# A hand-woven schedule for a two-layer graph network: seeds, round matrices, switch, clearing and loads get places in the tables

## What is computed

```python
# layer 0
mask = adj > 0
h  = relu((x @ W1a)[:, :, None, :] + (x[:, :, None, :] - x[:, None, :, :]) @ W1b + b1)
hm = einsum('bjkh,bjk->bjh', h, mask)
x  = layernorm(x + hm @ W2 + deg[..., None] * b2)
# layer 1
m   = relu(relu(x @ W1g + b1g) @ W2g + b2g)
msg = relu(adj @ m)
gi, gh = msg @ W_ih.T + b_ih, x @ W_hh.T + b_hh
r, z = sigmoid(i_r + h_r), sigmoid(i_z + h_z)
n = tanh(i_n + r * h_n)
x = layernorm(x + (1 - z) * n + z * x)
```

## Time and profile before

| | |
|---|---|
| median of three runs | 1038.85 us |
| the profiled execution's own time | 1039.86 us |
| its span, first to last instruction | 1038.2 us |
| mean granted TensorE clock | 0.95 |
| TensorE / VectorE / ScalarE / GpSimd busy | 86% / 83% / 54% / 30% |

### The profile page before, as it was taken

One profiled execution on the slowest core, in us unless ns is written; L12 is line 12 of the kernel. 1 busy time (PEld: TensorE's weight loads), 2 busy tenths in 40 slices (PEclk: granted clock), 3 DMA queues, 4 the chain that ended last, 5 costly groups with the idle time before them and its releaser, 6 DMA issues.

```text
span 1038.2 us, 25022 instructions
## 1 busy us (share of the span) xinstructions
PE 894.2 (86%) x10099; PEld 611.8 (59%) x10132; DVE 864.7 (83%) x1055; ACT 563.9 (54%) x1627; POOL 312.8 (30%) x300
## 2 busy tenths in 40 slices
PE   2778888989898998989899898989989898999874
PEld 1446666556666665666666566666666566666542
DVE  5489999898889888898988889888888988888643
ACT  3434355674656557555556656555665646555342
POOL 2101021331415142241525233142523314142341
PEclk9779999999999999999999999999999999999986
DMA  3131221222121211212121121212112221111000
GB/s 125 26 98 42 62 52 28 62 52 73 42 67 43 63 37 51 73 42 70 40 82 41 28 72 42 82 27 83 42 37 63 52 72 42 38 42 27 1 11 22
DMA packets 31426, 53.28 MB, mean 51 GB/s; under 512 B 8137, under 2 KB 16972, under 8 KB 31308
## 3 DMA queue, kind: packets, MB, share of 16 engines
q1 hardware_dynamic: 31308, 51.65, 19.3%
...
## 4 chain that ended last, share of the span: by engine, by line
PE 54%; ACT 17%; DVE 11%; issue 8%; POOL 5%; SPq 2%; another core or an unknown queue 1%; DMA 0%; POOLq 0%; DVEq 0%
PE PS L768 12%; PE PS L777 8%; DVE AC L1079 4%; DVE AC L1090 3%; PE PS L851 3%; ACT AM L1363 3%; PE PS L834 3%; PE PS L621 3%; ACT YO L1324 2%; POOL st L1469 2%; PE PS L754 2%; ACT AC L1410 2%; PE PS L642 2%; ACT AM L1364 2%; PE PS L608 2%
## 5 line engine op out<-in xcount | busy, mean ns | idle before, releaser
L1090 DVE SCALAR_TENSOR_TENSOR AC<-PS,AC 128x1152 f32<-128x1152 f32 (+1 forms) x288 | 351.4, 1220 | 73.8 <-PE PS L768 69.5
L1079 DVE SCALAR_TENSOR_TENSOR AC<-PS,AC 128x1152 f32<-128x1152 f32 (+1 forms) x288 | 350.9, 1218 | 55.1 <-PE PS L777 37.6
L768 PE MATMUL PS<-DM,VA 128*128 128x192 fp8e5 (+1 forms) x1152 | 137.6, 244 | 19.3 <-DVE AC L1079 8.2
L768 PE MATMUL PS<-DM,VB 128*128 128x192 fp8e5 (+1 forms) x1152 | 139.0, 245 | 0.0
L777 PE MATMUL PS<-DM,VB 128*64 128x192 fp8e5 (+1 forms) x1152 | 98.2, 252 | 41.1 <-DVE AC L1090 40.9
L768 PEld LDWEIGHTS PS<-DM,VA 128*128 128x128 f16 x1152 | 91.7, 101 | 40.8 <-DVE AC L1079 17.8
L1526 POOL MEMSET AC<- 128x768 f32 x32 | 23.7, 740 | 283.4 <-DVE DM L1060 268.7
L777 PEld LDWEIGHTS PS<-DM,VB 128*64 128x64 f16 x1152 | 43.5, 110 | 108.3 <-issue 50.5
L777 PE MATMUL PS<-DM,VA 128*64 128x192 fp8e5 (+1 forms) x1152 | 100.1, 255 | 0.0
L768 PEld LDWEIGHTS PS<-DM,VB 128*128 128x128 f16 x1152 | 77.5, 100 | 38.2 <-issue 3.2
L1533 POOL TENSOR_TENSOR AC<-AC,NNB 128x512 f32<-128x512 f32 x64 | 68.9, 1097 | 64.0 <-ACT AC L1410 64.0
...
## 6 DMA issues: line engine op xcount, KB each, us to landing
CW<-WM SPq DMA_DIRECT2D x128, 160.0 KB, 2.8
...
VA<-VN SPq DMA_DIRECT2D x64, 96.0 KB, 2.2
VB<-VN SPq DMA_DIRECT2D x64, 96.0 KB, 2.2
...
```

The source lines that it names most:

```text
L768: last = e.matmul(PS[:, b + i % 2, 256 * (i // 2) + cols.start:256 * (i // 2) + cols.stop], lhs[:, GRAPH[i], 0:128], d[:, i, :], start=Fal ...
L1079: e.scalar_tensor_tensor(dst, tiles(PS[:, b:b + 3, :])[:, :, cols], 0.0, dst, ALU.max, ALU.add).then_inc(s["sx"], 1)
L1090: e.scalar_tensor_tensor(dst, tiles(PS[:, b:b + 3, :])[:, :, cols], 0.0, dst, ALU.max, ALU.add).then_inc(s["sy"], 1)
```

## The change

Every piece of fixed work gets a letter or digit of its own, and the tables get a string more, for the gap ahead of B1: `0` and `1` are dgen 0 and 1 of the next quad, `2`, `3` and `4` those of this stage's, `s` seeds, `w` switch, `c` clear, `l` load. All four tables are new. Only the order of instructions in each engine's queue changes, and with it which of the two spare banks a piece gets.

```diff
--- before.py
+++ after.py
@@ -55,14 +55,15 @@
 ORDER = (
-    ("pe", "pte", "p", "te", "prt", "t", "pr", "re", "pe", "er", "pd", "pd", "pe", "pd", "pe", "d", "e", "r"),
...
+    ("ps2p3", "pe", "t", "t", "", "dtr", "e", "pdrpe", "", "ert", "pee", "ep", "4d", "p", "pre", "", "cwpd", "r", "e01"),
+    ("sp2d3", "pp", "", "t", "d", "tpp", "", "4tept", "n", "dp", "d", "p", "dc", "nld", "d0wpd", "", "epd", "p", "d1r"),
 )
...
@@ -482,8 +483,6 @@
             do("dgen", 0, 1)
             do("clear", 0)
             for t in range(NQ + 1):
-                if t < NQ:
-                    do("seeds", t)
                 link["t"] = tail(t - 2) if t > 1 else iter(())
                 if t % 2 == 0:
                     link["e"], link["d"] = link["d"], link["n"]
@@ -496,34 +495,39 @@
                 if t == NQ:
                     link["n"] = layer1_steps(do, bank, NG - 1)
                 order = ORDER[t % 2] if t < NQ - 1 else LAST[t - NQ + 1]
+
+                def between(codes):
+                    for c in codes:
+                        if c in "01":
+                            do("dgen", t + 1, int(c))
+                        elif c in "234":
+                            do("dgen", t, int(c))
+                        elif c == "s":
+                            do("seeds", t)
+                        elif c == "w":
+                            do("switch", t)
+                        elif c == "c":
+                            do("clear", t + 1)
+                        elif c == "l":
+                            if t // 2 + 2 < NG:
+                                do("load", t // 2 + 2)
+                        else:
+                            next(link[c], 0)
+
+                between(order[0])
                 for n in range(1, 10):
                     if t:
                         do("round_b", t - 1, n)
                     if t == NQ and n == 8:
                         do("flag")
-                    if n == 1:
-                        do("dgen", t, 2)
                     if t == 0 and n == 3:
                         next(link["r"])
                     if t == 0 and n == 8:
                         do("bias")
-                    for c in order[2 * n - 2]:
-                        next(link[c], 0)
+                    between(order[2 * n - 1])
                     if t < NQ:
                         do("round_a", t, n)
-                    if n in (2, 5):
-                        do("dgen", t, 3 if n == 2 else 4)
-                    if t < NQ and n == 8:
-                        do("dgen", t + 1, 0)
-                    if t < NQ and n == 9:
-                        do("switch", t)
-                        do("dgen", t + 1, 1)
-                    if t + 1 < NQ and n == 5:
-                        do("clear", t + 1)
-                    if t % 2 and n == 4 and t // 2 + 2 < NG:
-                        do("load", t // 2 + 2)
-                    for c in order[2 * n - 1]:
-                        next(link[c], 0)
+                    between(order[2 * n])
                 finish(link["p"])
                 finish(link["t"])
             link = {"t": tail(NQ - 1), "n": link["n"], "d": link["d"]}
```

More of the change, by code:

```diff
@@ L58 @@
 ORDER = (
-    ("pe", "pte", "p", "te", "prt", "t", "pr", "re", "pe", "er", "pd", "pd", "pe", "pd", "pe", "d", "e", "r"),
-    ("pe", "pd", "pe", "t", "pd", "t", "t", "t", "pd", "pd", "pd", "pd", "pn", "pd", "pd", "d", "n", "rd"),
+    ("ps2p3", "pe", "t", "t", "", "dtr", "e", "pdrpe", "", "ert", "pee", "ep", "4d", "p", "pre", "", "cwpd", "r", "e01"),
+    ("sp2d3", "pp", "", "t", "d", "tpp", "", "4tept", "n", "dp", "d", "p", "dc", "nld", "d0wpd", "", "epd", "p", "d1r"),
 )
 LAST = (
-    ("te", "d", "te", "dt", "t", "dd", "n", "ddn", "d", "nd", "nd", "d", "n", "d", "nd", "d", "n", ""),
-    ("td", "ee", "te", "tdd", "te", "dde", "nd", "nd", "de", "nde", "nde", "nd", "d", "n", "", "n", "dd", "nd"),
+    ("23st", "dt", "e", "tt", "de", "dnw", "d", "nd", "", "d", "d", "ndn", "d4d0", "nd", "d", "", "d1n", "", "n"),
+    ("t", "d", "e", "etd", "23e", "n", "tetedd", "d", "nddd", "d", "dned", "enne4", "", "", "", "nn", "dd", "", "dnd"),
 )
```

## The result

Beside each other on one chip, the kernel after took 966.2 us (four runs, 966.1 to 968.0) and the one before 1039.8 us (1038.7 to 1043.5). The ratio is 0.9291, with a 95% interval of 0.9264 to 0.9317. The forecast was 1006 us with a range of 990 to 1040: the direction was right, the gain is more than twice the forecast, and the time lies outside the range.

The account below looks back on a forecast made before the run. The kernel was taken as bound by how the TensorE and VectorE queues interlock. Pairs 2.28 us shorter, 29.6 over 13, and the ends summed to -32.4, giving 1006 us; range 990 to 1040.

Parts of the forecast that it names:

- by order alone the change brings 0.5 us a pair: Steady pairs of stages: reordering the queues alone takes a pair from 56.3 to 55.8 us.
- the rest of the gain is the clock: TensorE after count: its longest wait falls from 2.04 to 1.0 us, the clock is kept, saving 2.7 us a pair.
- The walk: VectorE and TensorE queues laid side by side by a start-time rule: a pair takes 56.3 us before, 55.8 after.
- 2.7 us missing between A6 and the end of the even stage: Part of the 3.5 us a pair left unexplained before, assigned to the stretch at the lower clock and what follows.
- R2: Rival: count's 1.0 us wait still lowers the clock; pair 59.0 us, kernel 1027 us; chance 0.20.
- port -0.75: At the turn, dgens beside GpSimd's multiplies take longer: a cost of 0.75 us a pair.
- The 0.85 us "unexplained": Rest of a pair's unexplained time, including ScalarE not ready for rank_ov (0.59 us); kept unchanged in the new pair.
- R5: Rival: the new order runs without extra waits, 55.8 to 56.1 us a pair, kernel 985 to 990; chance 0.10.
- R3: Rival: each dgen at the turn waits for a whole GpSimd operation, 4.6 us a pair, kernel 1057; chance 0.10.
- The turn: From one stage to the next: A1's add starts at T+5.05 and T+6.5, waiting for PE, no longer for GpSimd.
- The ends: Stages outside the 13 pairs: t=30 -1.2, t=2 -1.3, t=31 and 32 -0.3 us, t=0, 1, 3 nothing.

Follow-up runs that it names:

- filler: Kernel before with eight idle 128x512 matmuls ahead of B7 in even stages, where TensorE waited 2.04 us; 1031.8 us, ratio 0.9916.
- pool_late: Kernel after with dgens of the turn ahead of the seeds in stages 4 to 30, so GpSimd multiplies behind them; 959.3 us, ratio 0.9232.
- split_after: Kernel after with six pieces of the wide rounds moved by half a round, spreading five lumps over both halves; 994.5 us, ratio 0.9557.
- ranks_split: Kernel before with rank_t and its neighbour behind A1 exchanged, so that rank_ov gets the other spare bank; 1031.5 us, ratio 0.9908.
- fixed_new: Kernel before with fixed work of stages 0 to 30 in the new tables' gaps, pieces and last two stages as before; 1044.6 us, ratio 1.0047.
- count_moved: Kernel before with only count moved, from behind A5 to behind A7 in even stages; 1041.1 us, ratio 0.9998.
- pieces_new: Kernel before with pieces of stages 0 to 30 in the new tables' gaps, fixed work and last two stages as before; 1003.7 us, ratio 0.9645.
- last_fixed: Kernel after with the pieces of stages 31 and 32 in their gaps of before, fixed work in the new gaps; 975.7 us, ratio 0.9384.

## Why the forecast was wrong

**The step that failed: "by order alone the change brings 0.5 us a pair", and the rest of the gain is the clock.** The clock did stay at 1.00, but filler prices it: 0.79 us a pair. Between filler (58.89, clock 1.00) and pool_late (54.47, clock 1.00, port removed) the orders alone differ by 4.4 us a pair. The walk gave 56.3 and 55.8 for them, so it was 2.6 too short for the old order and 1.3 too long for the new. I had seen 2.7 us missing between A6 and the end of the even stage, saw a slow stretch there, and gave all of it to the clock; 3.4 us at 0.56 can't hold that much, as my own 1.7 in R2 said. With the clock at 1.00 the stretch still takes 7.2 us (t=6 of before), where it took 8.2 with the fall and 5.5 by the walk: 1.0 was the clock and 1.7 was the walk's.

In the terms of the forecast: clock 2.7, order 0.5, port -0.75 a pair; measured 0.8, 4.4 and -0.43. The 1.9 us too many for the clock hid half of the 3.9 us that the order lacked. That the pair came out 2.5 us off and not 4.4 is luck.

**What the walk lacked.** It priced each PE piece once, 52.3 us a pair in both orders. Measured, the same matmuls took 53.6 (filler, clock 1.00) and 51.8. The rows after show one source, the halves of a round and their neighbours. Columns are here those of the weights, the second number in `128*64`:

```profile
425.17 0.49 PE L772 MATMUL PS<-DM,VA 128*128 128x192 fp8e5 x4
425.59 0.36 PE L781 MATMUL PS<-DM,VA 128*64 128x192 fp8e5 x4
425.78 0.33 PE L781 MATMUL PS<-DM,VB 128*64 128x192 fp8e5 x4
426.04 0.50 PE L772 MATMUL PS<-DM,VB 128*128 128x192 fp8e5 x4
426.38 0.64 PE L646 MATMUL PS<-BDC,GT 128*128 128x128 f32 x4
426.86 1.00 PE L855 MATMUL PS<-SO,OT 128*128 128x64 f32 x8
427.70 0.49 PE L772 MATMUL PS<-DM,VA 128*128 128x192 fp8e5 x4
```

VA's 64-column group takes 0.19 us, start to start (425.59 to 425.78), where VB's 64-column group follows; where a 128-column piece follows, such groups take 0.28. The last output piece takes 0.84 in front of VA's 128-column group (426.86 to 427.70) and 1.04 before (480.34 to 481.38), in front of a 64-column one:

```profile
480.06 0.36 PE L777 MATMUL PS<-DM,VA 128*64 128x192 fp8e5 x4
480.34 1.10 PE L851 MATMUL PS<-SO,OT 128*128 128x64 f32 x8
481.38 0.36 PE L777 MATMUL PS<-DM,VB 128*64 128x192 fp8e5 x4
```

TensorE: Matmul & The Clock Gate in the Trainium skill ("Why this matters for your kernels") says that small matmuls, with under 128 columns of weights, can be placed so that each lands in its own column group of the array, and take less time together. Whether that happens here no run shows; two 64-column groups in a row are cheaper by the first rows, but of the six such places in this pair three took 0.19 us and three 0.36, which may hold a wait too short to be listed. split_after, with six pieces moved, raised PE's own time by 0.9 us at the same clock.

The neighbours are not all of the 1.8 us, and how it divides is not settled. Over half lies in the twelve wide 128-column groups of VB: 5.19 us in t=6 and 7 of before, 4.18 in t=14 and 15 of after. In both kernels `rank_ov` follows such a group, which takes 0.50 us before, where a listed wait comes between, and 0.34 after, where none does: the neighbour is the same, and the wait makes the difference. An estimate from these traces: if every group is given the shortest time seen with a neighbour of the same width, the two orders differ by 0.85 us, and the other 1.0 comes with waits.

**The 0.85 us "unexplained".** It was real and order can remove it: ranks_split took 0.6 of it away at equal clock. That was R5's argument, to which I gave 0.10. R5's time (985 to 990) was still 20 us too high.

**The shared port.** Mechanism right: the dgens went from 65.9 to 80.8 us, 1.15 a pair, and most of that was covered. Net 0.43 by pool_late, 0.75 forecast. R3 (4.6 a pair) is refuted; fixed_new has the same rise (79.1 us), and it gained nothing.

**`count`.** Forecast: PE wait 1.0, clock kept; measured 0.91 and 1.00. R2 is refuted. But the reason that I gave, a wait too short to lower the clock, is not shown. The clock fell in count_moved with no wait over 0.80 us from t=6 on, it stayed in pieces_new with one of 1.24, and before it stayed once with 2.04. The move itself is worth 0.2 us a pair in either order at a clock of 1.00 (58.92 to 58.69, 55.11 to 54.89).

**The turn.** A1's add was forecast at T+5.05 and T+6.5, no longer waiting for GpSimd; it starts at T+5.25 and T+6.28 (472.56-467.31, 445.38-439.10). The times are right, the way there is not: B1's add starts 0.6 and 0.5 us later than forecast (T+3.98 and T+5.02, behind the slower dgens), and A1's add follows it without a wait, where a wait for PE was forecast. From A2 on the walk of the even stage was late: A2 8.5 against 8.0, A4 14.3 against 13.8, B7 21.3 against 20.5, the next T 27.3 against 26.68, and in the odd stage 28.5 against 28.21.

**The ends.** t=30: -1.2 forecast, -2.0 measured. t=2: -1.3 forecast, -1.8 measured, but t=3 gave back 1.6 where I had put nothing. t=31 and 32: -0.3 forecast, -8.6 measured, the largest error outside the pairs. In the kernel before, the turn into t=32 on VectorE, on TensorE and as a stretch was:

```profile
971.32 1.18 DVE L1066 TENSOR_SCALAR SW<-CW 128x512 bf16<-128x512 uint16 x1
...
974.46 1.36 DVE L1090 SCALAR_TENSOR_TENSOR AC<-PS,AC 128x1152 f32<-128x1152 f32 x1 [1.69 <-PE PS L768]
```

```profile
972.61 0.38 PE L768 MATMUL PS<-SW,VA 128*128 128x128 bf16 x4 [2.83 <-DVE SW L1066]
```

```profile
970.00:974.00 4.00, 1.39 (x15) 1.02 (x16) 2.77 (x4) 0.00 (x0) 2.28 (x2) 0.86 0.00 0
```

`switch` (0.28 us on average elsewhere) lasted 1.18 there, GpSimd at work for 2.28 of the 4 us, PE had nothing for 2.83 us, and the clock was 0.86 in these 4 us. B1's add started 4.0 us after A9's (970.46). After, with `switch` in round 3:

```profile
903.99 0.95 DVE L1083 SCALAR_TENSOR_TENSOR AC<-PS,AC 128x768 f32<-128x768 f32 x1
907.03 1.36 DVE L1094 SCALAR_TENSOR_TENSOR AC<-PS,AC 128x1152 f32<-128x1152 f32 x1 [2.09 <-PE PS L772]
```

That is 3.0 us, 1.0 less. By last_fixed all the fixed work in `LAST` makes 4.2 us, 2.3 of them in these two stages; the larger share, 9.5 us (7.5), is the places of the pieces in the last two stages, which I did not take apart.

**The sum.** Of the 41.4 us between -32.4 and -73.8, the pairs are 32.7 (57.4 against 54.89: 0.9 the new walk itself, and 0.85 unexplained and 0.75 port that were put on top of it), t=31 and 32 8.3, t=30 0.8, the last stretch 1.1, and the start -1.5. That the pair's missing time was taken for the slow clock also kept the range away from 966.
